# Sums and folds of a gated cross-attention kernel in pairs of 16-bit parts, with parts of its order of work rewritten

## The reference

```python
def xattn(query, key, value):            # query = layernorm(x), key = value = ctx
    Q, K, V = query @ Wq.T + bq, key @ Wk.T + bk, value @ Wv.T + bv   # in 16 heads of 32
    attn = softmax(Q K^T / sqrt(32))
    out = (attn @ V) with the heads joined
    expert = (out @ We[e].T + be[e]).mean over the 8 e
    return expert @ Wo.T + bo

def ffn(x):                              # 8 classes, capacity 100
    probs = softmax(x @ w_gate); best = argmax(probs)
    place = running count of tokens with the same best
    rows with place < 100: probs[best] * (x @ w_expert + b_expert); the others: 0

x = x + tanh(g_xattn) * xattn(layernorm(x), ctx, ctx)
x = x + tanh(g_ffn) * ffn(layernorm(x))
```

## Time and profile before

| | us |
|---|---|
| median of 3 runs | 416.38 (416.18 to 416.67) |
| the profiled execution, its own time | 416.97 |
| its span, first to last instruction | 415.5 |
| PE busy | 405.2 (98%) |
| DVE busy | 332.8 (80%) |
| ACT busy | 227.6 (55%) |
| POOL busy | 166.2 (40%) |
| mean busy share of the DMA engines, prologue (24 to 62 us) | 0.99 |

### The profile page before, as it was taken

The page is one execution under the profiler, slowest core; times in us unless marked ns, Lnnn a source line. Parts: engine busy times, 40 slices in busy tenths (PEclk is TensorE's granted clock), DMA queues, the critical chain, the costliest instruction groups (busy, mean ns, idle before and its releaser), DMA issues.

```text
span 415.5 us, 8770 instructions
## 1 busy us (share of the span) xinstructions
PE 405.2 (98%) x3122; PEld 191.7 (46%) x3122; DVE 332.8 (80%) x678; ACT 227.6 (55%) x318; POOL 166.2 (40%) x153
## 2 busy tenths in 40 slices
PE   8999999999999999999999999999999999999996
PEld 4566564444444344444434443443444444354442
DVE  7439346886797889988988998899896688579994
ACT  5435322569466754947585585748556473785100
POOL 2029999015080247309033530803261072550460
PEclk9999999999999999999999999999999999999999
DMA  8999971365058407723960683286059026231683
GB/s 266 340 390 396 390 291 35 89 120 161 2 113 184 174 0 163 213 96 88 174 208 2 141 227 101 65 175 232 2 128 235 6 51 175 71 115 34 118 175 137
DMA packets 64853, 63.19 MB, mean 152 GB/s; under 512 B 41225, under 2 KB 44437, under 8 KB 64811
## 3 DMA queue, kind: packets, MB, share of 16 engines
q1 hardware_dynamic: 59667, 56.18, 48.9%
q0 software_dynamic: 1632, 3.49, 3.1%
q10 hardware_dynamic: 3512, 2.97, 2.1%
HBM read 29.59 MB, written 12.98 MB: 102 GB/s over the span
## 4 chain that ended last, share of the span: by engine, by line
PE 78%; DVE 9%; POOL 4%; issue 4%; DMA 2%; ACT 1%; SPq 0%; DVEq 0%; POOLq 0%; ACTq 0%
PE ps L828 60%; PE ps L449 10%; PE ps L398 3%; PE ps L580 3%; DVE bn_raw L1450 2%; POOL known L1893 1%; POOL std L1902 1%; POOL rstd L1893 1%; DMA raw<-in_L_xattn_Wk_dram 1%; DMA q_stack<-shift 1%; DVE base_cnt L1619 1%; DVE rows L1789 1%; ACT xb L1215 1%; DVE bn_raw L1540 1%; DVE xb L1534 1%
## 5 line engine op out<-in xcount | busy, mean ns | idle before, releaser
L1215 ACT ACTIVATE probs<-ps 120x1024 f32<-120x1024 f32 x64 | 62.0, 1023 | 22.6 <-PE ps L828 22.6
L1568 DVE TENSOR_REDUCE neg_max<-ps 128x16 bf16<-128x1920 f32 x32 | 68.6, 2144 | 4.1 <-PE ps L828 4.1
L1952 POOL TENSOR_TENSOR attn_lo<-attn,attn_hi 128x512 f16<-128x512 f32 x28 | 31.8, 1157 | 95.9 <-ACT attn_hi L1215 95.9
L828 PE MATMUL ps<-xnT_hi,wqT_hi 128*128 128x512 f16 x128 | 48.6, 380 | 0.0
L828 PE MATMUL ps<-mixT_hi,attn_hi 128*128 128x512 f16 x128 | 48.6, 380 | 0.0
L828 PE MATMUL ps<-mixT_lo,attn_hi 128*128 128x512 f16 x128 | 48.5, 379 | 0.0
L828 PE MATMUL ps<-xnT_lo,wqT_hi 128*128 128x512 f16 x128 | 48.5, 379 | 0.0
L1960 POOL TENSOR_TENSOR xb<-xb,mix_bias 128x512 f32<-128x512 f32 x32 | 39.6, 1270 | 18.7 <-DVE cb_col L1511 18.7
L1215 ACT ACTIVATE q_hi<-ps,bias_cols 128x512 f16<-128x512 f32 x32 | 22.0, 687 | 35.3 <-PE ps L828 35.3
L828 PE MATMUL ps<-q_stack,k_stack 97*120 97x512 f16 x128 | 34.7, 390 | 0.9 <-DMA q_stack<-shift 0.8
L828 PE MATMUL ps<-probs,den_sel 120*32 120x256 f32 x512 | 34.1, 384 | 0.0
(11 more groups left out here) (270 smaller groups left out, 791.7 us busy)
## 6 DMA issues: line engine op xcount, KB each, us to landing
xb<-in_x_dram SPq DMA_DIRECT2D x8, 1024.0 KB, 6.0
q_stack<-q_hi SPq DMA_DIRECT2D x48, 128.0 KB
out_dram<-xb SPq DMA_DIRECT2D x6, 1024.0 KB, 6.0
raw<-in_L_xattn_We_dram SPq DMA_DIRECT2D x5, 1024.0 KB, 11.1
q_stack<-q_lo SPq DMA_DIRECT2D x32, 128.0 KB
xb<-in_L_xattn_We_dram SPq DMA_DIRECT2D x3, 1024.0 KB, 10.4
k_stack<-k_scratch SPq DMA_DIRECT2D x8, 360.0 KB, 4.3
out_dram<-xb SPq DMA_DIRECT2D x8, 256.0 KB, 2.1
```

The lines of the kernel that those rows point to most:

```text
L828: return e.matmul(out_, a, b, start=start, stop=stop, **kw)
L1215: return e.activation(out_, in_, func, **kw)
L1568: e.tensor_reduce(neg_max[:, :, :, g], quad[:, :, 0:NT * SK].rearrange("p j (t s) -> p t j s", t=NT), AX.X, ALU.max, negate=True).then_inc ...
L1952: e.tensor_tensor(attn_lo[:, g, :], attn[:, g, :], attn_hi[:, g, :], ALU.subtract).then_inc(s_alo, 1)
```

## The change

1. **be_unit:** the expert biases are split in two 16-bit parts (`be_part_high` on ACT, `be_part_low` on DVE, both ahead of the third Wv turn's evacuation) and summed by eight 16-bit matmuls in place of four fp32.
2. **w_gate:** it is loaded straight in its turned layout (128 x 4 x 8, runs of eight floats); `gate_rows_unit`, its eight transposes, is gone. DVE sums it in `gate_over`, which waits for that load.
3. **wogT, fold, bias_part, mix_bias, gateT:** evacuated as pairs (ACT high, DVE low) and multiplied in 16 bit. Before, each had only an ACT evacuation. The fold of gateT in `gate_mix` too.
4. **Order of the prologue:** `v_unit(0)` stands ahead of the turns of Wo; `gate_out_unit` stands behind the first two `x_unit`s. Some units wait for fewer semaphores (the last `v_unit`, the four `mix`).
5. **places:** behind `q_end` in rounds 0 to 5; DVE runs `choose` ahead of `logit_scale`, and `read_places` one `x_lo` later. For the seventh batch the places go to another bank, so that PE no longer waits for the table and `x1`.
6. **Shift row of the last batch:** its DMA is issued by SP, ahead of the stores of two tiles.
7. **Last round:** `table_values` ahead of the third `weight_sums`; the last batch's logits in 16-bit parts (a new `part_high` on ACT and `part_low` on DVE), behind `mix_high` of the last tile. The seventh batch keeps fp32 logits.
8. **Last tile:** product, `last_out` and store in two halves of 256 columns.

```diff
@@ prologue
-            unit("be_col", col, [(s_const, 16 * N_CONST), (s_set, 5)],
-                 act=lambda e, b: e.activation(be_hi[:, :], b[:, 0:NK], ACT.Copy, scale=BIAS_SCALE / NE), dve=parts)
+            unit("be_col", col, [(s_be, 18), (s_set, 6)],
+                 act=lambda e, b: e.activation(be_hi[:, :], b[:, 0:NK], ACT.Copy), dve=parts)
...
             unit("wogT", pe, needs_of("wg_mean") + [(s_wt["woT"][i], 16) for i in range(NK)],
-                 act=lambda e, b: e.activation(partT[:, :], b[:, :], ACT.Copy))
+                 **pair_evac(*wog_parts, lambda b: b[:, :], GATE_SCALE))
+
+        def fold_parts(e, b):
+            for k in range(NK):
+                for part in wog_parts:
+                    ins = e.matmul(b[:, k * NE:(k + 1) * NE], part[:, k * P:(k + 1) * P], gate_sum16[:, NE:2 * NE],
+                                   start=(part is wog_parts[0]), stop=(part is wog_parts[1]))
+            return ins
...
-                unit(("mix", k), pe, needs_of(*[("woT", o) for o in range(NK)]) + [(s_sumh, 1), (s_suml, k + 1)]
+                unit(("mix", k), pe, [(s_suml, k + 1)]
...
             unit("gateT", pe, needs_of("wog", "mix_bias") + [(s_ws, NE - 1)],
-                 act=lambda e, b: e.activation(partT[:, :], b[:, :], ACT.Copy, scale=gate_scale[:, 0:1]))
+                 act=lambda e, b: e.activation(part_hi[:, :], b[:, :], ACT.Copy, scale=gate_scale[:, 0:1]),
+                 dve=lambda e, b: e.scalar_tensor_tensor(out=part_lo[:, :], in0=b[:, :], scalar=gate_scale[:, 0:1],
+                                                         in1=part_hi[:, :], op0=ALU.mult, op1=ALU.subtract))
...
-        k_units(1, [gate_rows_unit, be_unit, gate_and_mean])
+        k_units(1, [be_unit, gate_and_mean])
         weight_units("wqT", pair=(wqT_hi, wqT_lo), scale=QK_SCALE)
+        v_unit(0)
         weight_units("woT", pair=(woT_hi, woT_lo), scale=OUT_SCALE)
-        v_unit(0)
         gate_out_rows_unit()
@@ PE, rounds
-                (places, -1, 0), (q_end, 1, 0), (values, 0, 2), (values, 0, 3), (max_scores, 1, 0),
+                (q_end, 1, 0), (places, -1, 0), (values, 0, 2), (values, 0, 3), (max_scores, 1, 0),
@@ PE, places of the seventh batch
-                if b == B - 2:
-                    e.wait_ge(s_x1, 4 * b + 3)
-                    e.wait_ge(s_tab, b)
-                elif b < B - 2:
+                if b < B - 2:
@@ SP, shift row
-                    if r < B - 2:
-                        e.wait_ge(s_sh, r + 2)
-                        load(q_stack[3 * DK:STACK, :, :, :].rearrange("o j g s -> o (j g) s"),
-                             shift[:, :], s_rsh)
+                    e.wait_ge(s_sh, r + 2)
+                    load(q_stack[3 * DK:STACK, :, :, :].rearrange("o j g s -> o (j g) s"),
+                         shift[:, :], s_rsh)
                     if r == B - 2:
                         store_tiles(r, (0, 1))
@@ PE, last round
-                (values, 0, 1), (scores, 0, 3), (weight_sums, 0, 2), (table_values, -1, 0), (value_sums, 0, 2),
+                (values, 0, 1), (scores, 0, 3), (table_values, -1, 0), (weight_sums, 0, 2), (value_sums, 0, 2),
...
-                (mix_high, 0, 2), (mix_low, 0, 2), (logits, 0, 0), (mix_high, 0, 3), (mix_low, 0, 3),
+                (mix_high, 0, 2), (mix_low, 0, 2), (mix_high, 0, 3), (logits, 0, 0), (mix_low, 0, 3),
```

More of the change, by code:

```diff
@@ L82 @@
 FAR = 1.0e6
+LAST_PARTS = [(t, slice(0, D)) for t in range(NT - 1)] + [(NT - 1, slice(h * D // 2, (h + 1) * D // 2)) for h in range(2)]
 def build(nc, x, ctx, g_xattn, g_ffn, Wq, bq, Wk, bk, Wv, bv, We, be, Wo, bo, w_gate, w_expert, b_expert, out):
@@ L353, in build @@
         s_ls = sem("s_ls")
[L355 to L356 removed]
+        SET, SETV, N_CONST = 16, 21, 1
+        be_parts = [a[0:NE, 1, :] for a in (sum_hi, sum_lo)]
+        bias_parts = [a[:, 0, :] for a in (sum_hi, sum_lo)]
+        wog_parts = [a[:, 2, :] for a in (sum_hi, sum_lo)]
         units, made, late = [], {}, []
@@ L565, in bias_part_unit, with pe @@
             unit("bias_part", pe, needs_of("be_col", "wog", *[("woT", k) for k in range(NK)]),
-                 act=lambda e, b: e.activation(partT[:, :], b[:, :], ACT.Copy))
+                 **pair_evac(*bias_parts, lambda b: b[:, :], 1.0 / OUT_SCALE))
         def mix_bias_unit():
-            unit("mix_bias", lambda e, b: e.matmul(b[:, :], ones_col[:, 0:1].to_broadcast([P, P]), partT[:, :],
-                                                   start=True, stop=True),
+            def pe(e, b):
+                for part in bias_parts:
+                    ins = e.matmul(b[:, :], ones_16[:, 0:1].to_broadcast([P, P]), part,
+                                   start=(part is bias_parts[0]), stop=(part is bias_parts[1]))
+                return ins
+            unit("mix_bias", pe,
                  needs_of("bias_part") + [(s_bo, 16)],
                  dve=lambda e, b: e.scalar_tensor_tensor(out=mix_bias[:, :], in0=b[:, :],
-                                                         scalar=1.0 / (DK * BIAS_SCALE * OUT_SCALE), in1=bo_bc[:, :],
+                                                         scalar=1.0 / (DK * BIAS_SCALE), in1=bo_bc[:, :],
                                                          op0=ALU.mult, op1=ALU.add))
@@ L922, in gate_mix @@
                         e.wait_ge(s_, n)
-                    fold(e, g0_b).then_inc(s_mg, 1)
+                    for k in range(NK):
+                        for part in (part_hi, part_lo):
+                            ins = mm(g0_b[:, k * NE:(k + 1) * NE], part[:, k * P:(k + 1) * P], gate_sum16[:, NE:2 * NE],
+                                     start=(part is part_hi), stop=(part is part_lo))
+                    ins.then_inc(s_mg, 1)
             def route2(bank, part, hi, lo):
@@ L1455, in moments1, with be_part_low, gate_over @@
                     e.bn_aggr(mv[:, b % 2, t, :], bn_raw[:, 0, t, :]).then_inc(s_mv1, 1)
+            def be_part_low():
+                e.wait_ge(s_be, 17)
+                e.scalar_tensor_tensor(out=be_parts[1], in0=be_sb[:, :], scalar=BIAS_SCALE / NE, in1=be_parts[0],
+                                       op0=ALU.mult, op1=ALU.subtract).then_inc(s_be, 1)
+            def gate_over():
+                e.wait_ge(s_wg, 16)
+                e.tensor_reduce(wg_over[:, :], wg[:, :, :].rearrange("p k e -> p e k"), AX.X, ALU.add).then_inc(s_wg, 1)
             def prepare(_, i):
@@ L1479, in _ @@
             for i in range(N_FIRST):
+                if units[i]["done"] == made[("wvT", 2)]:
+                    be_part_low()
+                    gate_over()
                 prepare(0, i)
```

115 lines of the change are left out of this document (59 added, 56 removed).

## The result

The changed kernel took 414.13 us (median of 21 executions, 412.54 to 415.93) beside 416.46 of the kernel before (21 executions, 415.88 to 417.06): ratio 0.9941, 95% interval 0.993 to 0.9952. That is 2.3 to 2.5 us faster where 4.0 were forecast, and 0.13 us above the range. The profiled execution took 413.09 (span 411.4 for 415.5), which is the 413.0 that the prediction's sum gave for it.

A forecast was written before the change was run, and what follows sets the result against it. PE was taken to bound the kernel (busy 405.2 of 415.5 us), with DVE binding near the end. Terms 0.2 + 0.6 - 0.74 + 0.59 + 2.8 + 0.7 - 0.6 + 0.4 = 3.95 gave 412.4 us, range 410.0 to 414.0.

The forecast's parts named there:

- late units: Units after the prologue: most of two issue waits on PE go as semaphore waits are struck, 0.6 us saved (0 to 0.8).
- part_lo: First weight sums: PE waits for DVE's new low part of gateT, ending near 95.0 us; 0.74 us lost.
- fold in gate_mix: gateT's fold on PE goes from 0.79 to 0.20 us in 16 bit; 0.59 us saved.
- places: Middle rounds: PE's wait of 0.56 us for base_cnt goes in five rounds; 2.8 us saved, bound below 1.4.
- opening: Last batch's start: shift-row and table waits go, a token-table wait comes, gathered-row stall goes; 0.7 us saved (0.3 to 1.9).
- last logits: Before the last places: DVE bounds and gains part_low's 0.62 us, PE's saving becomes waiting; 0.6 us lost.
- halves: Last tile: half-size matmuls, a shorter last DVE output and half the bytes stored; 0.4 us saved (0 to 0.6).
- The wait for wog: Prologue behind the fold: wog ready near 56.4 us, PE asks at 55.95; 0.45 us lost.
- rival C: TensorE drops to its lower clock at four new waits, 1.7 us each, 6.8 in all: 419.2 us; chance 0.03.
- the four waits: New PE waits: 2.2 us at the fold, 0.74 at first weight sums, 1.25 at token table, 1.3 at last places.
- A: Rival: ACT is not in the way in the prologue, 1.3 to 2.5 us come through: 410.5 us; chance 0.22.
- the 2.7 us: Upper bound of the prologue's saving if ACT's chain were not in the way; 0.2 us was forecast.

The follow-up runs named there:

- e2_store_later: Changed kernel with ACT's second store_k (twelve k_scratch issues) behind wogT's evacuation and the last batch's logits back in fp32; 410.26 us, ratio 0.9846.
- e2_before_places: Kernel before with only the places moved behind q_end in the middle rounds, choose and read_places reordered on DVE; 413.44 us, ratio 0.993.
- e4_longer: Changed kernel with two more xn-sized ACTIVATE on ACT ahead of xn, lengthening PE's wait before the fold; 416.29 to 418.51 us in five executions without the stall.
- e1_after_again: Changed kernel run again unaltered; 413.13 and 413.95 us at full clock, 414.47 and 415.86 at 0.995 and 0.996, two executions with the stall.

## Why the prediction was right in its sum and wrong in its time

The sum, at the full clock. I cut both traces at the same seven instructions (the rows of PE ending in a count are of the chain, whose starts lie up to 0.2 behind those of the timeline).

The changed kernel:

```profile
11.49 2.43 PE ps L456 x12
...
64.41 12.19 PE ps L840 x104
...
94.28 15.90 PE ps L840 x161
```

```profile
129.33 0.17 PE L840 MATMUL ps<-gate_sum,part_hi 128*128 128x16 f16 x1
...
311.21 0.17 PE L840 MATMUL ps<-gate_sum,part_hi 128*128 128x16 f16 x1
...
365.04 1.29 DVE L1559 TENSOR_TENSOR attn<-ps,attn 128x512 f32<-128x512 f32 x2 [1.02 <-PE ps L840]
...
395.04 0.19 PE L840 MATMUL ps<-choice,tri 128*128 128x32 bf16 x1 [1.70 <-DVE base_cnt L1650]
```

The kernel before, where no earlier row has the place (the others are in the earlier trace rows):

```profile
11.36 2.43 PE ps L449 x12
...
64.64 12.19 PE ps L828 x104
```

```profile
314.74 0.17 PE L828 MATMUL ps<-gate_sum,part_hi 128*128 128x16 f16 x1
...
369.36 1.29 DVE L1528 TENSOR_TENSOR attn<-ps,attn 128x512 f32<-128x512 f32 x2 [1.02 <-PE ps L828]
```

| stretch | before | after | saved | forecast |
|---|---|---|---|---|
| first K unit to the last V unit's end | 53.28 | 52.92 | 0.36 | 0.2 |
| to the first weight sums (late units, part_lo) | 29.67 | 29.87 | -0.20 | 0.6 - 0.74 = -0.14 |
| to the second round's logits (fold in gate_mix) | 35.66 | 35.05 | 0.61 | 0.59 |
| five rounds, to the seventh's logits (places) | 184.77 | 181.88 | 2.89 | 2.8 |
| to the division of the last values (opening) | 54.62 | 53.83 | 0.79 | 0.7 |
| to the last places (last logits) | 29.40 | 30.00 | -0.60 | -0.6 |
| to the end of the span (halves) | 16.74 | 16.36 | 0.38 | 0.4 |

Together 4.23; the first K unit started 0.13 later, which leaves the 4.1 between the spans. The executions' own times differ by 3.9, because 1.69 us lie outside the span now and 1.47 did before. Every stretch comes out near its forecast, the two against the change too.

But the agreement of the first is partly luck. By the starts of the matmuls PE came to the fold (before) or to the x turns in its place (after) 1.59 us earlier, for 1.70. It waited 1.73 before the fold, for 2.2, and then 0.57 behind it, which had no term. The wait for wog, forecast at 0.45, did not come: wog is ready at 55.65 and not at 56.4. In the second stretch the units gave 0.68 up to gateT's unit and the way from there cost 0.89, for 0.6 and 0.74.

part_low cost DVE 0.60 in its dense stretch, while PE's own saving there became waiting, and undoing it gave it back: in `e2_store_later` the same stretch takes 392.36 - 362.97 = 29.39 again. At the opening of the last batch the table's wait came, 1.0 in the profile after. That the shift row's wait went is not shown to be the work of SP: it stands in ten of the fourteen other traces with the new order, 0.3 to 0.9, and there the table has only 0.5 to 0.2 left; and it is absent from `e2_before_places`, where ACT still issues that DMA. Whichever comes, PE goes on at about the end of the same DVE instruction (place_hot), as forecast.

What failed. First, small: I took the profiled execution to stand 0.6 above the median after as before. The thirteen executions of the changed kernel that kept the clock (ten of the 21, three of the later ones) have a median of 413.02, just under the profiled one. So the full-clock gain over 416.46 is 3.4, and 412.4 should have been 413.0. Of that 0.6 the 0.2 outside the span is in every execution of every kernel with the new code (1.68 to 1.88 us, for 1.45 to 1.57), and the sum had no term for it. Nor had it one for the start: in three traces with the old prologue the first K unit starts at 10.90 to 11.20 us, in the fifteen with the new one at 10.93 to 13.51, eight of them at 11.59 or later. I had put the new loads at nothing; no run takes them back, so whether they are the reason stays open.

Second, and this put the time outside the range: **rival C**. Its mechanism was right, and its size fits the one fall measured in the unaltered kernel (1.7 for 1.7), though it was put together from other rows and the fall in `e4_longer` cost 2.6. I gave it 0.03 because I had put it as a fall at each of the four waits in every execution, and my only row against it was one: after 1.0 us of waiting the pace holds. I used that row to clear a wait of 2.2. What happened is a fall at one wait of the four, in some executions: 17 of the 30 without the stall lost the clock, median 414.91, against 413.02 of the others. The difference of 1.9 is the 1.7 of the fall and leaves 0.2 for the longer wait, which cost 1.0 in the one such execution seen.

In the 21 executions of the result eleven lost the clock, just over half, so the median is no longer 413.0 but the third fastest of the slower group, 414.13. Where the clock fell is seen in one of the 17, before the V unit behind the fold; for the others it is argued, from the seven kernels without a wait of 1.6 there: of their 29 executions without the stall 28 have a clock of 0.998 or more, and the clock of the other fell at the start. The wait of 1.7 before the last places never brought the clock down in any trace here, nor did the 1.0 and the 0.8, nor 1.59, 1.63 and 1.74 before the fold. The falls seen outside the stall stand behind 2.16 and 2.17 there and 2.5 at the start; no run tells what lies between. Nor is it shown that the length of the wait alone decides which executions fall: of the unaltered changed kernel three have a trace, one of them fallen, and its wait was the longest.

Third, the reason for the spread: I wrote that the wait is about 2.2 from issues that took 0.6 each, and took them as fixed. The eleven behind the last woT_hi took 5.79 to 6.86 us in the three profiles of the unaltered changed kernel, and the forecast wait is that of the execution in which the clock fell. So this wait is the one term of the sum that is not a number but a band of 1 us. In the kernel before the same issues ended 0.4 earlier and cost nothing: the fold started at 51.61, 0.25 after wogT was there. The change took the work in front of the fold away and left ACT's chain as the bound. The prediction saw that step (A falls: the 2.7 us did not come), but not that a bound made of DMA issues carries their spread into the time.

What it means for the change: the whole of it gives 2.4 us, and the places alone give 3.1. The rest, pairs of parts included, adds some 0.3 at the full clock (3.4 against 3.1, on two chips; between the first K unit and the end the traces have 0.6) and loses more than that at the fold. With the issues moved behind the evacuation, and the last logits left in fp32, the kernel takes 410.26.

## What to carry to other kernels

Where an edit turns PE's work into waiting, ask not only whether the end moves but how long PE then stands idle in one place, and whose pace sets that: if it is a chain of DMA issues, the wait has a spread, and the median follows the executions in which the clock falls. Look at the clock of every execution, not at the profiled one alone, before trusting a sum made on one trace. Keep DMA issues off the engine whose next result the matrix engine needs; here moving twelve of them behind one evacuation gave about 2 us at the full clock and ended the falls.

## What I had not expected of the hardware

That one wait can bring the clock down in some executions of a kernel and leave it up in others, with 0.5 us of idle time between the two (1.63 and 2.17) and turns a little stretched in front, and that the fall is not one price: eight matmuls of 512 columns at 0.43 instead of 0.216 in `e1_after_again`, twelve and more in `e4_longer`. The granted clock of the records does not tell everything: it stands at 1.00 over the first 10 us of both kernels, though the six matmuls from 1.05 us on start 0.43 apart there. And the pace of one engine's DMA issues varies by 1 us over eleven issues between executions of the same kernel with everything ahead of them equal to 0.02 us (the last `woT_hi` starts at 41.58 and 41.56).
